# Batch 1's choice: tile flags added in pairs on VectorE and the last four sums on TensorE

## The reference

```
x = x + tanh(g_xattn[0]) * attention(layernorm(x), ctx, mask)      # 77 context rows
x = x + tanh(g_ffn[0])   * experts(layernorm(x))

def experts(x):                                # 8 experts, hidden size 2048
    probs = softmax(einsum('ntd,ed->nte', x, gate_w))
    g, m = top_k(probs.transpose(0, 2, 1), 512)   # each expert chooses 512 tokens
    xin = x[batch_idx, m]
    h = gelu(einsum('nekd,edf->nekf', xin, w1))
    h = einsum('nekf,efd->nekd', h, w2)
    return zeros.at[batch_idx, m].add(g[..., None] * h)
```

## Time and profile before

| | us |
|---|---|
| median of 3 runs | 1564.37 (1562.61 to 1566.11) |
| the profiled execution, its time | 1563.59 |
| its span from first to last instruction | 1561.8 |
| busy in it: TensorE | 1493.4 |
| VectorE | 1015.7 |
| ScalarE | 732.8 |
| GpSimd | 593.7 |

### The profile page before, as it was taken

How to read it: one execution, slowest core, us unless ns; L and a number is a source line. 1 busy time by engine, 2 the same in 40 slices (tenths; PEclk the granted TensorE clock), 3 DMA queues, 4 the chain that set the end, 5 groups by cost and what they waited for, 6 DMA issues and landing times.

```text
span 1561.8 us, 22316 instructions
## 1 busy us (share of the span) xinstructions
PE 1493.4 (96%) x7169; PEld 1211.2 (78%) x7169; DVE 1015.7 (65%) x1716; ACT 732.8 (47%) x1347; POOL 593.7 (38%) x554
## 2 busy tenths in 40 slices
PE   6886699999999999999999999999999999999996
PEld 5654477787788888888888888888888888888885
DVE  2578776657766676676657676767667675766542
ACT  1385233445444554454445444455445444554432
POOL 2265555543544044323443244403531444323211
PEclk9999699999999999999999999999999999999998
DMA  7176423543333333245234423334324433442133
GB/s 229 55 255 204 162 88 99 141 138 82 89 120 62 101 97 95 93 88 116 82 108 81 110 91 99 74 95 103 100 76 95 110 96 93 82 108 81 42 78 70
DMA packets 101401, 163.58 MB, mean 105 GB/s; under 512 B 7411, under 2 KB 45315, under 8 KB 101285
## 3 DMA queue, kind: packets, MB, share of 16 engines
q1 hardware_dynamic: 86885, 128.50, 26.4%
q0 software_dynamic: 14400, 33.56, 11.9%
HBM read 128.48 MB, written 33.55 MB: 104 GB/s over the span
## 4 chain that ended last, share of the span: by engine, by line
PE 86%; DVE 7%; issue 2%; ACT 2%; POOL 1%; DMA 1%; POOLq 0%; SPq 0%; DVEq 0%; ACTq 0%
PE bank L1325 42%; PE bank L1211 33%; PE bank L1185 4%; PE bank L1480 2%; PE bank L572 1%; PE bank L590 1%; PE bank L400 1%; DVE st L817 1%; DVE onehot L1366 1%; ACT xT L641 1%; DVE sc L793 0%; DMA ctx_raw<-in_ctx 0%; PE bank L1355 0%; DVE w2hl L1170 0%; DVE hid_low L1203 0%
## 5 line engine op out<-in xcount | busy, mean ns | idle before, releaser
L1325 PE MATMUL bank<-w2hl,hh 128*128 128x512 f32 x2048 | 635.7, 392 | 0.0
L1211 PE MATMUL bank<-xo,whl 128*128 128x512 f32 x2352 | 543.0, 390 | 3.7 <-DVE mix L1275 2.8
L1211 PEld LDWEIGHTS bank<-xo,whl 128*128 128x128 f32 x2352 | 440.7, 188 | 98.5 <-DVE mix L1275 3.7
L1325 PEld LDWEIGHTS bank<-w2hl,hh 128*128 128x128 f32 x2048 | 380.4, 188 | 76.0
L1325 PE MATMUL bank<-w2hl,hid_low 128*128 128x512 f32 x1024 | 398.7, 389 | 0.0
L1325 PEld LDWEIGHTS bank<-w2hl,hid_low 128*128 128x128 f32 x1024 | 192.2, 188 | 40.4
L1430 POOL DMA_INDIRECT layer_out<-y,slot_row x64 | 103.2, 1613 | 301.8 <-ACT y L1345 287.0
L1170 DVE TENSOR_TENSOR w2hl<-raw,w2hl 128x512 fp32r<-128x512 f32 x213 | 147.7, 715 | 50.6 <-ACT w2hl L1165 41.3
L1139 POOL TENSOR_TENSOR whl<-raw,whl 128x512 fp32r<-128x512 f32 x56 | 82.1, 1466 | 258.2 <-ACT whl L1105 258.2
L1165 ACT ACTIVATE w2hl<-raw 128x512 fp32r<-128x512 f32 x228 | 136.5, 624 | 60.1 <-DMA raw<-in_L_ffn_w 43.9
L1144 POOL TENSOR_TENSOR whl<-wsum,whl 128x512 fp32r<-128x512 f32 x56 | 75.1, 1341 | 183.4 <-ACT whl L1126 183.4
(11 more groups left out here) (224 smaller groups left out, 1783.0 us busy)
## 6 DMA issues: line engine op xcount, KB each, us to landing
raw<-in_L_ffn_w SPq DMA_DIRECT2D x228, 256.0 KB, 2.7
raw<-in_L_ffn_w SPq DMA_DIRECT2D x72, 512.0 KB, 4.9
x_s<-in_x SPq DMA_DIRECT2D x8, 1024.0 KB, 6.9
layer_out<-x SPq DMA_DIRECT2D x8, 1024.0 KB, 9.0
xn_rows<-xn SPq DMA_DIRECT2D x8, 1024.0 KB, 4.9
raw_k<-in_L_xattn_Wk SPq DMA_DIRECT2D x1, 1024.0 KB, 5.4
raw_q<-in_L_xattn_Wq SPq DMA_DIRECT2D x1, 1024.0 KB, 11.3
raw_v<-in_L_xattn_Wv SPq DMA_DIRECT2D x1, 1024.0 KB, 13.4
```

The lines of the kernel that those rows point to most:

```text
L1211: last = pe.matmul(bk[:, :], whl[:, p % 2, part, 2 * w + k, :], xo[:, xpart, x, k, :], start=(not adds and k == 0 and part == HIGH and xpa ...
L1325: last = pe.matmul(Y_BANKS[c][:, :], high if hpart == HIGH else low[:, c * P:(c + 1) * P], w2hl[:, f % 4, part, :], start=(s == 0 and hpar ...
```

## The change

For batch 1, the one `tensor_reduce` over sixteen tiles becomes two `tensor_tensor` additions on VectorE, in place in `atleast`: tiles 8 to 15 are added to tiles 0 to 7 (448 values on each partition), then tiles 4 to 7 to tiles 0 to 3 (224 values). TensorE then sums the four remaining tiles with four matmuls of 56 columns in place of one. It is the loop of batch 0, with 4 steps for 16. Batch 0 stays as it is, and so does the piece's place in every queue. The second addition waits for the first on VectorE's own semaphore.

```diff
                 if b == 0:
                     reach.then_inc(bit_count, 1)
                 else:
+
                     step(reach)
-                if b == 1:
-                    tile_counts(dve, count[:, :, :], atleast[:, :, :, :].rearrange("p c t e -> p c e t"))\
-                        .then_inc(bit_count, 1)
+                    for half in (TB // 2, TB // 4):
+                        fold = dve.tensor_tensor(atleast[:, :, 0:half, :], atleast[:, :, 0:half, :],
+                                                 atleast[:, :, half:2 * half, :], ALU.add)
+                        if half == TB // 4:
+                            fold.then_inc(bit_count, 1)
+                        else:
+                            step(fold)
...
                 total = CHOICE_BANK[:, 0:CANDS * E]
-                if b == 0:
-                    for t in range(TB):
-                        last = pe.matmul(total.rearrange("p (c e) -> p c e", c=CANDS), ones_m[:, :],
-                                         atleast[:, :, t, :],
-                                         start=(t == 0), stop=(t == TB - 1))
-                else:
-                    last = pe.matmul(total, ones_m[:, :], count[:, :, :].rearrange("p c e -> p (c e)"),
-                                     start=True, stop=True)
+                tiles = TB if b == 0 else TB // 4
+                for t in range(tiles):
+                    last = pe.matmul(total.rearrange("p (c e) -> p c e", c=CANDS), ones_m[:, :],
+                                     atleast[:, :, t, :],
+                                     start=(t == 0), stop=(t == tiles - 1))
                 last.then_inc(bit_total, 1)
```

## The result

| | us |
|---|---|
| before, median of 6 runs | 1563.55 |
| changed, median of 6 runs | 1571.07 (1569.93 to 1572.72) |
| ratio (95% interval) | 1.0052 (1.0040 to 1.0063) |
| the changed kernel's profiled execution, its time and span | 1572.72 and 1570.9 |

The ratio stands for about 8 us, more than 0.2% and outside the forecast range of 1563.0 to 1568.6. (One of the six runs of before was a disturbed one of 1906.81 us; the ratio leaves it out.)

A forecast was written before the change was run, and what follows sets the result against it. TensorE, busy 96% of the span, was taken as the bound. Waits after 2.94, less waits before 2.01, plus matmuls 0.79 made +1.7 us on 1564.37: 1566.1 us, with eight in ten between 1563.0 and 1568.6.

The forecast's parts named there:

- the 2.01 us of waits that could be won: TensorE's waits before the count matmuls of pieces 0, 2, 4, 6 and 8, all a faster count could give back.
- the folds' lengths: VectorE's two additions, undisturbed: 0.40 and 0.27 us, together 0.67, by the rate of bf16 operands.
- their turns with GpSimd: Odd pieces: each fold waits for a GpSimd operation, one L1133 between them; matmul starts 2.75 us after L899 ends.
- the waits of 0.40 in pieces 3 to 9: TensorE in pieces 3, 5, 7 and 9 waits 0.40 us each for the later count, 1.60 us together.
- piece 0: First count matmul: at 189.80 us in place of 189.87, so TensorE's wait is 0.62 us.
- Rivals 1 (no turn): Folds not held up: -1.2 us, 1563.2; if only GpSimd's turn between them goes: -0.6 us, 1563.8. Chance 0.18.
- 2 (f32 rate): VectorE's folds run at the f32 rate, 0.62 and 0.38 us: total +3.7 us, 1568.1. Chance 0.13.
- 3 (a lost race): In odd pieces L899 starts behind GpSimd's L1170, some 1.2 us later: +5 to +6 us, 1570 to 1571. Chance 0.04.
- rival 4 (dearer matmuls): Added TensorE matmuls cost more than 0.026 us each through weight loads: a few tenths. Chance 0.03, shared with something else downstream.
- the end of the sum: Behind 252 us, after the choice's stage, the shift of +1.7 us passes to the end at its full size.
- The price of the added matmuls: Thirty more 56-column matmuls on TensorE at 0.026 us each: 0.79 us, all on the path.
- something else downstream: Unpriced case of an effect behind the choice; chance 0.03, shared with rival 4 (dearer matmuls).

The follow-up runs named there:

- the 98 pairs: The changed kernel with 98 tiny matmuls and their weight loads added at TensorE's start; 1564.65 us, ratio 1.0012 against before.
- the memsets: The kernel before with 20 one-value memsets added at VectorE's start, TensorE's stream untouched; 1566.84 us, ratio 1.0029.
- with the folds: The kernel before with both additions, then a reduction of the remaining four tiles and one matmul as before; 1572.22 us, ratio 1.0062.

## Why the prediction was wrong

**What held.** What bounds the choice's stage, the 2.01 us of waits that could be won, the folds' lengths (0.40 and 0.27 predicted, 0.39 and 0.27 measured), their turns with GpSimd, the waits of 0.40 in pieces 3 to 9 and 0.72 in piece 1 (0.40 and 0.68), none in even pieces, 0.026 us a matmul. Expert 0 grew by 1.7 us, with the whole changed kernel as with the loop's position mended. Only piece 0 was off, to either side (0.62 predicted; 0.45 in the changed kernel, 0.72 with the 98 pairs). By these terms, 2.72 - 2.01 + 0.78, the changed kernel's trace has 1.5 of its 1.7 us. The last 0.2 is in none of them (half of it came ahead of the first count, where TensorE's granted clock was at the lower level for 4.1 us in place of 3.9), so that its total met 1.7 exactly is in part luck; with the 98 pairs the terms are 2.99 - 2.01 + 0.78 = 1.8 for a measured 1.7. Holding GpSimd back confirmed the mechanism that carried it. Rivals 1 (no turn), 2 (f32 rate) and 3 (a lost race) didn't happen, and rival 4 (dearer matmuls) didn't either: thirty took 0.78 us for 0.79.

**The step that failed** is the end of the sum: "Behind 252 us ... I let the shift pass to the end at its full size". It looked for what the later code waits for, and held it to be tied to TensorE's own progress. It left out that thirty matmuls are also sixty instructions in a stream that is fetched in blocks, and that a loop of four taken branches stands behind them. The price of the added matmuls was given as 0.79 us, their time on TensorE; it was 0.79 plus 6.1 us in the loop. That sixty instructions alone, on a kernel that computes as before, cost 5.8 us, and that 196 more take all but 0.6 us of the loss away again, shows it. The range failed with it: every rival with a price was a mechanism inside the choice, and "something else downstream" had a share of 0.03 and no price.

**Could the profile of before have told?** In part. The page lists two instruction queues with 69 and 47 packets, and the prediction passed them by. The records of the branches and of queue q8 show a fetch behind each taken branch, of 3.6 to 4.0 us, which was almost hidden: the matmuls already queued covered 3.66 us of it. That the cover was thin could be read; on which side of the threshold 60 more instructions would land needs the count of instructions from the loop's start to the end of its block, which the views don't give. A fair forecast would have kept the centre and widened the range upwards by what four uncovered fetches cost.

**Open.** Why the packets behind a branch come as two with some 3.3 us between them, why a fetch takes 3.4 us one time and 4.5 another, and how large TensorE's window is, was not tested. Nor was why VectorE's gaps are smaller with the memsets than with the folds, though both kernels have 20 instructions more (its second standstills last 2.2 to 3.2 us with the memsets, 3.1 to 3.7 with the folds). The changed kernel's 10 more VectorE instructions are not shown to cost anything: with TensorE's position mended it lost no more than expert 0's part.

## What to carry to other kernels

Ahead of a loop whose branch is taken with the engines full, every added instruction can have a second price, its place: before believing that a local edit costs or gains a few us, compare the parts of the span that hold nothing of it, and look there for waits on "issue" just behind the branches. To separate the two, pad the stream by whole blocks, at a time when the engine waits anyway, and see what remains. And a reduction on VectorE isn't always the slow choice beside a busy GpSimd: an addition of two SBUF operands in its place takes turns with GpSimd, and two of them take two turns.

## What the runs showed of the hardware

- With nothing but 60 instructions more ahead of its loop TensorE lost 5.8 us over four taken branches; with 30 or 90 more nothing (one execution each). 256 more (the changed kernel with 98 pairs) brought back all but 0.6 us of the loss.
- Behind a taken branch TensorE's first instruction came 3.4 to 4.5 us later where its block had to be fetched and 0.3 us where it hadn't; in this loop 3.66 us of it were covered by queued matmuls.
- TensorE's instructions come in packets of 16 KB, and a shift of 128 mended VectorE's stream. That its packets are among those of 8 KB is likely but not shown: they are on the only other instruction queue, so other engines' packets are there too. With the loop well placed TensorE fetched 33 packets in the run in place of 69, none of them inside the loop.
- A fold of 448 bf16 values lasts 0.39 us alone and 1.36 behind GpSimd's L1170; one of 224 lasts 0.27 alone and 1.25 when GpSimd's next instruction got in first, each time though VectorE was free for some 0.04 us only.
- In four of the fourteen profiled executions TensorE's granted clock was at the lower level for 3.4 us behind an idle time of 1.8 us that all have; it cost 1.4 to 1.5 us each time.
- The time from the start to the choice varies by 3.8 us among the profiled executions (first L1185 from 180.6 to 184.4 us), more than most effects looked for here; lengths within the trace are steadier than totals.
